# Gate o of an LSTM: its own PSUM bank and its own tanh, 1 + o on VectorE

## The chip, the cores and the metric

One core of a Trainium2 chip runs the whole program. The metric is the device time of one execution in microseconds (us), lower is better.

## The reference

The input x is (4, 64, 56, 56). Four stages follow, each with a residual: a layer norm over channels and an involution (7x7, 4 groups, kernels made from the pixel by two 1x1 convolutions); a top-2 mixture of 16 experts (SwiGLU, hidden 128); a 3x3 convolution; and an LSTM-like recurrence over the 3136 tokens of each of the 4 images, of which only this matters here:

```python
    def step(carry, xs):
        h, c = carry
        i_t = jax.nn.sigmoid(xi_t + h @ V_i)
        g_t = jnp.tanh(xg_t + h @ V_c)
        o_t = jax.nn.sigmoid(xo_t + h @ V_o)
        c_new = h * c + i_t * g_t
        h_new = o_t * jnp.tanh(c_new)
        return ((h_new, c_new), h_new)
    (_, _), hs = lax.scan(step, (h0, c0), (xi, xf, xg, xo))
```

(f_t is computed and not used.) Each token needs the h of the token before, so the 3136 steps can't overlap.

## The kernel before, in words

The image is worked off row by row, 56 rows of 56 pixels, 4 images side by side. All engines run the same schedule: a loop over rows whose body is unrolled over the 56 pixels t. In each step t an engine first does its part of the recurrence for pixel t of row j - 6 (LAG), and then its "fill", a piece of another stage for row j (pe_fill, act_fill, dve_fill). Which piece stands in which step is written by hand in main_places. Six head rows without recurrence come first, and the last six rows have no involution. Queues are in order; waits are semaphores, whose values are computed into registers (act_registers, fill_registers, pe_registers) inside the loop.

One step of the recurrence goes so. sigmoid(z) is (1 + tanh(z/2)) / 2, the halves are folded into the weights, and h is carried in two f16 digits: HR, and H5, the rest.

- TensorE (pe_row): when HR is written (hd1_done), three products VW x HR, for the gates g, i and o; when H5 is written (hd2_done), three products VB x H5. The first of each three is L1330, whose weights are loaded ahead, the two others are L1400. All add to one PSUM bank, GATES[c] (c = 0 for the first 28 pixels, 1 for the others), which already holds bias and input parts. The last product counts gates_done.
- ScalarE: L732 takes tanh of all three gates into G6 (4 images x 3, 12 elements). L736 then computes 1 + o twice into O5 (o1_done), and when the cell is there (cell_done) L739 takes tanh of it into TC5 in PSUM.
- VectorE (dve_row): L968, a scan, computes the cell from G6 and ADD3; then fill_registers; L975 takes the reciprocal of 1 + o when o1_done is there (rec_done); L979 writes HR = (1 + o) tanh(c); L982, a scan that needs the reciprocal, writes H5; L985 writes h to HIST; L987 the next ADD3.

The bias and input parts of the gates come from "prefill", nine products for each half row: three biases (L1116) and six input parts (L1120). Half 0 is prefilled in steps 51 to 54 (PRE0), half 1 in steps 3 and 6 (PRE1_AT). In step 6 a convolution tap (CONV, L1301) stands behind the prefill in TensorE's queue, in step 54 the duplication of the experts' input (DUP, L1158).

The experts' first product goes to bank H1B (H1, steps 12, 17, ..., 47) and is read by SI one step later; their second to H2B; the routing weights, spread by four products (L1269) in steps 14, 19, ..., 49, to bank DB, from which ScalarE copies them to DBS (L692) two steps later (the last time one step later). DB also takes the spread of the norm's scales (spread_rs, L1131, steps 10 and 11), copied by ScalarE in step 12 (RSC). L814 (RED, step 7) and L861 (DPLO, step 11) are fills of VectorE that work on 32 partitions beginning at 64 and at 32.

## Time and profile before

| what | value |
|---|---|
| three runs | 4000.49, 4002.73, 4004.25 us (median 4002.73) |
| the profiled execution, its own time | 4000.67 us |
| its span, first to last instruction | 3998.9 us |
| granted TensorE clock, mean | 0.517 |
| PE / PEld / DVE / ACT / POOL busy | 90 / 66 / 85 / 63 / 54 % |
| chain that ended last | PE 66%, DVE 14%, ACT 13%, issue 5%, POOL 1% |
| idle of ScalarE before L732, until TensorE's L1400 | 1195.7 us in 3073 of 3136 steps |
| idle of VectorE before L968, until L732 | 243.2 us in 874 steps |
| from 1000 to 2000 us: PE, PEld, DVE, ACT, POOL busy | 914, 676, 861, 652, 566 us, clock 0.50 |

The span is about 196 us of head rows and 3800 us of the loop, which looks the same from row to row. TensorE's busy share is high because its fills run while the recurrence is at ScalarE and VectorE; a matmul's record includes its latency, so that 90% isn't full use.

### The profile page before, as it was taken

What the parts mean: (1) busy time and instruction counts of PE and PEld (TensorE: products, weight loads), DVE (VectorE), ACT (ScalarE), POOL (GpSimd) and SP (SyncE); (2) the same over time, 40 slices, a digit from 0 to 9 for tenths busy, and PEclk for the clock granted to TensorE, in tenths of its full rate; (3) what the DMA queues carried; (4) which work ended last, traced back from release to release, by engine and by line L of the source; (5) the groups of instructions that cost most, each with busy time, mean ns of one, the idle gap of its engine ahead of it and who ended that gap; (6) DMA issues with size and microseconds to landing.
All of it is one profiled execution on the core that took longest, in us unless ns stands there. A gap on an engine that the chain in (4) does not pass through costs nothing.

```text
span 3998.9 us, 130353 instructions
## 1 busy us (share of the span) xinstructions
PE 3586.2 (90%) x35548; PEld 2658.7 (66%) x35548; DVE 3382.6 (85%) x21828; ACT 2526.5 (63%) x11666; POOL 2159.1 (54%) x3173
## 2 busy tenths in 40 slices
PE   6799999999898999999999999999989899988887
PEld 5666666666666666666666666666666666666665
DVE  6788888888888888888888888888888888887787
ACT  3366666666666666666666666666666666666565
POOL 6655565656565656555555555565655565652222
PEclk7955555555555555555555555555555555555555
DMA  5000000000000000000000000000000000000000
GB/s 74 2 1 1 1 1 1 1 1 1 1 1 1 1 1 1 1 1 1 1 1 1 1 1 1 1 1 1 1 1 1 1 1 1 1 2 1 1 1 1
DMA packets 44537, 11.06 MB, mean 3 GB/s; under 512 B 39913, under 2 KB 44010, under 8 KB 44490
## 3 DMA queue, kind: packets, MB, share of 16 engines
q1 hardware_dynamic: 42378, 10.05, 1.6%
q10 hardware_dynamic: 2112, 0.46, 0.1%
q8 instruction: 20, 0.33, 0.0%
q14 instruction: 27, 0.22, 0.0%
HBM read 7.29 MB, written 3.21 MB: 3 GB/s over the span
## 4 chain that ended last, share of the span: by engine, by line
PE 66%; DVE 14%; ACT 13%; issue 5%; POOL 1%; DVEq 0%; DMA 0%; ACTq 0%; POOLq 0%
PE GATES L1330 14%; PE YB L1150 10%; PE GATES L1400 9%; ACT O L736 7%; PE H1B L1144 7%; ACT G L732 6%; DVE O L975 6%; PE YB L1301 6%; PE TAPB L1137 6%; PE DB L1269 5%; DVE HR L979 5%; PE DB L1131 3%; PE H2B L1177 1%; PE H1B L1177 1%; PE H2B L1125 1%
## 5 line engine op out<-in xcount | busy, mean ns | idle before, releaser
L732 ACT ACTIVATE G<-GATES 128x12 f32<-128x12 f32 x3136 | 572.3, 182 | 1207.0 <-PE GATES L1400 1195.7
L1400 PEld LDWEIGHTS GATES<-HR,VW 128*128 128x128 f16 x6272 | 419.9, 106 | 605.7 <-issue 560.0
L968 DVE TENSOR_TENSOR_SCAN CT<-G,CT 128x12 f32<-128x12 f32 x3136 | 587.1, 187 | 268.0 <-ACT G L732 243.2
L1330 PE MATMUL GATES<-HR,VW 128*128 128x4 f16 x3136 | 532.2, 170 | 307.2 <-DVE HR L979 213.9
L736 ACT ACTIVATE O<-G 128x8 f32<-128x8 f32 x3136 | 662.1, 211 | 98.9 <-ACT G L732 0.2
L975 DVE RECIPROCAL O<-O 128x4 f32<-128x4 f32 x3136 | 567.5, 181 | 177.2 <-ACT O L736 0.2
L1396 PEld LDWEIGHTS <-VW 128*128 128x128 f16 x3136 | 457.4, 146 | 353.8 <-issue 317.2
L1400 PE MATMUL GATES<-H,VB 128*128 128x4 f16 x6272 | 616.8, 169 | 0.0
L987 DVE SCALAR_TENSOR_TENSOR CT<-HIST,CT 128x4 f32<-128x4 f32 x3136 | 521.4, 166 | 108.8
L1400 PE MATMUL GATES<-HR,VW 128*128 128x4 f16 x6272 | 613.1, 168 | 0.0
L1150 PE MATMUL YB<-HD,W 128*64 128x112 f32 x3840 | 595.5, 412 | 2.1 <-DVE HD L856 2.1
L530 POOL TENSOR_TENSOR HD<-VV,DBS 128x448 f32<-128x448 f32 x392 | 444.0, 1133 | 277.8 <-ACT DBS L692 277.8
L982 DVE TENSOR_TENSOR_SCAN H<-O,CT 128x20 f16<-128x20 f32 x3136 | 590.1, 188 | 0.0
L523 POOL TENSOR_TENSOR PA<-PA,XN 128x336 f32<-128x336 f32 x350 | 294.2, 841 | 446.7 <-ACT PA L659 446.7
L739 ACT ACTIVATE CT<-CT 128x8 f32<-128x8 f32 x3136 | 508.0, 162 | 40.0
L1330 PE MATMUL GATES<-H,VB 128*128 128x4 f16 x3136 | 525.4, 168 | 0.0
L979 DVE SCALAR_TENSOR_TENSOR HR<-O,CT 128x4 f16<-128x4 f32 x3136 | 498.4, 159 | 1.1
L1137 PE MATMUL TAPB<-RED,WT 128*128 128x112 f16 x2636 | 434.0, 283 | 2.2 <-DVE PD L842 2.0
L1144 PE MATMUL H1B<-XS,WM 128*128 128x224 f16 x1920 | 425.0, 375 | 0.0
L1144 PE MATMUL H2B<-XS,WM 128*128 128x224 f16 x1920 | 424.7, 375 | 0.2
L985 DVE TENSOR_TENSOR HIST<-O,CT 128x4 f32<-128x4 f32 x3136 | 415.8, 133 | 0.0
L1400 PEld LDWEIGHTS GATES<-H,VB 128*128 128x128 f16 x6272 | 414.7, 105 | 0.1
(242 smaller groups left out, 6995.0 us busy)
## 6 DMA issues: line engine op xcount, KB each, us to landing
out_dram<-OUT SPq DMA_DIRECT2D x112, 28.0 KB, 1.9
X<-in_x_dram SPq DMA_DIRECT2D x4, 672.0 KB, 11.3
STG<-in_L_ffn_w_dram SPq DMA_DIRECT2D x4, 512.0 KB, 12.5
U<-in_L_conv_U2s_dram SPq DMA_DIRECT2D x1, 972.0 KB
W<-in_L_ffn_w_dram SPq DMA_DIRECT2D x1, 512.0 KB, 11.7
X<-in_x_dram ACTq DMA_DIRECT2D x4, 112.0 KB, 3.0
S<-in_L_conv_S1s_dram SPq DMA_DIRECT2D x1, 108.0 KB
S<-in_L_conv_S2s_dram SPq DMA_DIRECT2D x1, 108.0 KB
```

The costliest lines, as they stand in the source:

```text
L732: act.activation(G6[:, :, 2:5], gates[c][:, w, :, :], ACT.Tanh, scale=1 / GSCALE).then_inc(step_in, 1)
L736: act.activation(O5[:, :, 1:5:3], G6[:, :, 3:4].broadcast_to([128, B, 2]), ACT.Copy, scale=O_MAX, bias=1.0)\
L968: dve.tensor_tensor_scan(CELL.rearrange("z b k -> z (b k)"), G6[:, :, :].rearrange("z b k -> z (b k)")[:, 0::2], ADD3.rearrange("z b k -> ...
L975: dve.reciprocal(O5[:, :, 3], O5[:, :, 1]).then_inc(rec_done, 1)
L979: dve.scalar_tensor_tensor(out=HR[:, :], in0=O5[:, :, 1], scalar=HSCALE, in1=TC5[:, :, 0], op0=ALU.mult, op1=ALU.mult)\
L982: dve.tensor_tensor_scan(H5[:, :, :].rearrange("z b k -> z (b k)"), O5[:, :, :].rearrange("z b k -> z (b k)"), TC5.rearrange("z b k -> z ( ...
L987: dve.scalar_tensor_tensor(out=ADD3[:, :, 2], in0=HIST[:, t, :], scalar=0.5, in1=CELL[:, :, 2], op0=ALU.mult, op1=ALU.mult).then_inc(step_ ...
L1137: last = pe.matmul(bank[:, m * TOK:(m + 1) * TOK], WT[:, i * K7 + j0 + m].rearrange("z p g c -> z (p g c)"), RED[:, :], start=(m == 0), st ...
L1144: last = pe.matmul(bank[:, m * 2 * TOK:(m + 1) * 2 * TOK], WM[:, which, part, EG * k + m, :], XS[:, :], start=(m == 0 and part == 0), stop ...
L1150: last = pe.matmul(YE[64 * p:64 * p + 64, :], W3[:, EG * k + m, :], HD[:, k % 2, m, p, :], start=first, stop=(k == NG - 1 and m == EG - 1) ...
L1330: return pe.add_instruction(mybir.InstMatmult(name=nc.get_next_instruction_name(), engine=mybir.EngineType.PE, start_tensor_calc=False, st ...
L1400: last = pe.matmul(gates[c][:, w, :, SLOT[g]], wt[:, g].rearrange("z m c -> z (m c)"), digit, start=False, stop=True, skip_group_check=True)
```

## The change

Gate o leaves the banks GATES and gets columns in bank DB (GATE_O, 112 columns for each half row), and OT, 4 more columns there, holds its tanh. Per step: TensorE counts gates_done after i's product with H5, the second of three, and gate_o_done after o's; ScalarE takes tanh of g and i into G6 (8 elements), then tanh of o into OT (4 elements, PSUM to PSUM), and L736 is gone; VectorE, behind the cell's scan, waits for OT and computes 1 + o twice into O5 (8 elements), and only then does its registers and the reciprocal.

Around it: the spread scales of the norm go to H2B and the routing weights to H1B instead of DB, so that H1 waits for the copy DBS (dbs_done) instead of SI, and H2 for the copy of the scales (rsc_done). The nine prefill products come in another order, o's three last: in step 6 for half 1 and in step 54 for half 0, and the first of them waits for o1_done of the same step. Since bank DB can't be cleared while it is in use, ScalarE writes zeros to the other half's GATE_O behind L739 in steps 1 and 49, and o's product with HR in steps 2 and 50 waits for that (oz_done). In the head rows DB is used as before.

```diff
-        PRE0={51: (0, 1, 2), 52: (3, 4), 53: (5, 6), 54: (7, 8)}, COPY=None, RSE=None)
+        PRE0={51: (0, 1), 52: (2, 3), 53: (4, 5), 54: (6, 7, 8)}, COPY=None, RSE=None)
...
-PRODUCTS = 3 + 2 * 3
-PRE1_AT = {3: (0, 1, 2, 3, 4), 6: (5, 6, 7, 8)}
-SLOT = (2, 0, 1)
+
+INPUTS = (("b", 0), ("b", 1), (0, 0), (0, 1), (1, 0), (1, 1), ("b", 2), (0, 2), (1, 2))
+PRODUCTS = len(INPUTS)
+FIRST_O = INPUTS.index(("b", 2))
+PRE1_AT = {3: (0, 1, 2, 3, 4, 5), 6: (6, 7, 8)}
+ZERO_AT = (1, 49)
+SLOT = (1, 0)
 MAIN, HEAD = main_places(), head_places()
...
-        gates = [g[:, 0:HALF * B * 3].rearrange("z (k b t) -> z t b k", b=B, k=3) for g in GATES]
+        gates = [g[:, 0:HALF * B * 2].rearrange("z (k b t) -> z t b k", b=B, k=2) for g in GATES]
+        GATE_O = [DB[:, c * TOK:(c + 1) * TOK] for c in range(2)]
+        gate_o = [g.rearrange("z (b t) -> z t b", b=B) for g in GATE_O]
+        OT = DB[:, 448:448 + B]
...
         def spread(lstm):
-            return DB if lstm else GATES[1]
+            return H2B if lstm else GATES[1]
+
+        def weights_bank(lstm):
+
+            return H1B if lstm else DB
 
...
-                act.activation(DBS[:, :], DB[:, 0:EG * 2 * TOK], ACT.Copy).then_inc(dbs_done, 1)
+                act.activation(DBS[:, :], weights_bank(lstm)[:, 0:EG * 2 * TOK], ACT.Copy).then_inc(dbs_done, 1)
...
                     act.wait_ge(gates_done, 1 + n + 1)
-                    act.activation(G6[:, :, 2:5], gates[c][:, w, :, :], ACT.Tanh, scale=1 / GSCALE).then_inc(step_in, 1)
+                    act.activation(G6[:, :, 2:5:2], gates[c][:, w, :, :], ACT.Tanh, scale=1 / GSCALE).then_inc(step_in, 1)
+                    act.wait_ge(gate_o_done, 1 + n + 1)
+                    act.activation(OT[:, :], gate_o[c][:, w, :], ACT.Tanh, scale=1 / GSCALE).then_inc(ot_done, 1)
                     act_registers(act, j, t, involution)
-
-                    act.wait_ge(step_in, 1 + 2 * n + 2)
-                    act.activation(O5[:, :, 1:5:3], G6[:, :, 3:4].broadcast_to([128, B, 2]), ACT.Copy, scale=O_MAX, bias=1.0)\
-                        .then_inc(o1_done, 1)
                     act.wait_ge(cell_done, 1 + n + 1)
                     act.activation(TC5[:, :, 0:4:3], CELL[:, :, 2:3].broadcast_to([128, B, 2]), ACT.Tanh, scale=0.5)\
                         .then_inc(t_done, 1)
+                    for k in range(2):
+                        if t == ZERO_AT[k]:
+
+                            act.wait_ge(o1_done, 1 + n + 1)
+                            act.activation(GATE_O[1 - k], CST[:, CZERO:CZERO + 1].broadcast_to([128, TOK]), ACT.Copy).then_inc(oz_done, 1)
                 act_fill(act, j, t, involution, lstm, experts, pre)
 
         def act_head_row(act, j):
...
+                    dve.wait_ge(ot_done, 1 + n + 1)
+                    dve.scalar_tensor_tensor(out=O5[:, :, 1:5:3], in0=OT[:, :].unsqueeze(2).broadcast_to([128, B, 2]), scalar=O_MAX,
+                                             in1=O5[:, :, 2:3].broadcast_to([128, B, 2]), op0=ALU.mult, op1=ALU.subtract)\
+                        .then_inc(o1_done, 1)
                     fill_registers(dve, j, t, involution, lstm, experts)
...
-        def prefill(pe, c, k):
-
-            if k < 3:
-                return pe.matmul(GATES[c][:, SLOT[k] * TOK:(SLOT[k] + 1) * TOK], BX[:, k].rearrange("z m c -> z (m c)"),
-                                 ONEH[:, :], start=(k == 0), stop=False, skip_group_check=True)
-            d, g = divmod(k - 3, 3)
+        def prefill(pe, c, k, lstm):
+
+
+            d, g = INPUTS[k]
+            bank = GATE_O[c] if g == 2 else GATES[c][:, SLOT[g] * TOK:(SLOT[g] + 1) * TOK]
+            if d == "b":
+                return pe.matmul(bank, BX[:, g].rearrange("z m c -> z (m c)"), ONEH[:, :],
+                                 start=(k == 0 or (k == FIRST_O and not lstm)), stop=False, skip_group_check=True)
             xs = X4S[:, :].rearrange("z (p q w) -> z p q w", p=2, q=Q)[:, :, :, c * HALF:(c + 1) * HALF]
-            return pe.matmul(GATES[c][:, SLOT[g] * TOK:(SLOT[g] + 1) * TOK].rearrange("z (q p t) -> z p q t", q=Q, p=2),
+            return pe.matmul(bank.rearrange("z (q p t) -> z p q t", q=Q, p=2),
...
                         if lstm:
-                            pe.wait_ge(dbs_done, 1 + NG * j)
+
+                            pe.wait_ge(ve_done, 1 + 2 * j + 2)
...
-                    last = prefill(pe, 1, k)
+                    if k == FIRST_O:
+                        pe.wait_ge(o1_done, 1 + (j - LAG) * W + t + 1)
+                    last = prefill(pe, 1, k, lstm)
                     if k == PRODUCTS - 1:
                         last.then_inc(pre1_done, 1)
             if experts and t in P.H1:
                 k = P.H1.index(t)
-                pe.wait_ge(si_done, 1 + NG * j + k)
+                if lstm:
+                    pe.wait_ge(dbs_done, 1 + NG * j + k)
+                else:
+                    pe.wait_ge(si_done, 1 + NG * j + k)
...
-                    pe.wait_ge(ve_done, 1 + 2 * j + 2)
+                    pe.wait_ge(rsc_done, 1 + j + 1)
...
-                    if lstm:
-                        pe.wait_ge(rsc_done, 1 + j + 1)
                     pe.wait_ge(dp_step, 1 + 3 * j + 3)
                 for m in range(EG):
                     for p in range(2):
-                        last = pe.matmul(DB[:, (2 * m + p) * TOK:(2 * m + p + 1) * TOK], SEL[:, p, EG * k + m, :], DP[:, :],
+                        last = pe.matmul(weights_bank(lstm)[:, (2 * m + p) * TOK:(2 * m + p + 1) * TOK], SEL[:, p, EG * k + m, :], DP[:, :],
...
-                    last = prefill(pe, 0, k)
+                    if k == FIRST_O and lstm:
+                        pe.wait_ge(o1_done, 1 + (j - LAG) * W + t + 1)
...
-                if experts:
+                if experts and lstm:
+                    pe.wait_ge(dbs_done, 1 + NG * (j + 1))
+                elif experts:
...
+            if t - 1 in ZERO_AT:
+                pe.to_reg(1 + 2 * (j - LAG) + ZERO_AT.index(t - 1) + 1)
...
-                pe.to_reg(1 + NG * j)
+                pe.to_reg(1 + 2 * j + 2)
...
+            if FIRST_O in PRE1_AT.get(t, ()) or FIRST_O in P.PRE0.get(t, ()):
+                pe.to_reg(1 + (j - LAG) * W + t + 1)
...
                         multiply_loaded(pe, gates[c][:, w, :, SLOT[0]], first, digit)
-                        for g in range(1, 3):
-                            last = pe.matmul(gates[c][:, w, :, SLOT[g]], wt[:, g].rearrange("z m c -> z (m c)"), digit,
-                                             start=False, stop=True, skip_group_check=True)
-                    last.then_inc(gates_done, 1)
+                        last = pe.matmul(gates[c][:, w, :, SLOT[1]], wt[:, 1].rearrange("z m c -> z (m c)"), digit,
+                                         start=False, stop=True, skip_group_check=True)
+                        if wt is VB:
+                            last.then_inc(gates_done, 1)
+                        if wt is VW and t - 1 in ZERO_AT:
+                            pe.wait_ge(oz_done, 1 + 2 * (j - LAG) + ZERO_AT.index(t - 1) + 1)
+                        last = pe.matmul(gate_o[c][:, w, :], wt[:, 2].rearrange("z m c -> z (m c)"), digit,
+                                         start=False, stop=True, skip_group_check=True)
+                    last.then_inc(gate_o_done, 1)
```

## Rows read from the trace of the kernel before

**Rows 1.** The page, the chain that ended last, shares of the span by engine

```profile
PE 66%; DVE 14%; ACT 13%; issue 5%; POOL 1%; DVEq 0%; DMA 0%; ACTq 0%; POOLq 0%
```

**Rows 2.** One line of the kernel, L732: duration ns min/median/max, first and last start

```profile
L732 ACT ACTIVATE G<-GATES x3136: 182/182/185, 196.2 to 3993.6; 128x12 f32<-128x12 f32 x196
```

**Rows 3.** Timeline of a quiet step (step 18 of a row): start us, duration us, instruction

```profile
2251.44 0.18 ACT L732 ACTIVATE G<-GATES 128x12 f32<-128x12 f32 x1 [0.61 <-PE GATES L1400]
2251.65 0.19 DVE L968 TENSOR_TENSOR_SCAN CT<-G,CT 128x12 f32<-128x12 f32 x1
...
2251.87 0.16 ACT L739 ACTIVATE CT<-CT 128x8 f32<-128x8 f32 x1
2251.89 0.18 DVE L975 RECIPROCAL O<-O 128x4 f32<-128x4 f32 x1
2251.95 0.54 ACT L687 ACTIVATE SI<-H1B 128x448 f32<-128x448 f32 x1
2252.07 0.16 DVE L979 SCALAR_TENSOR_TENSOR HR<-O,CT 128x4 f16<-128x4 f32 x1
...
2252.14 0.19 DVE L982 TENSOR_TENSOR_SCAN H<-O,CT 128x20 f16<-128x20 f32 x1
2252.25 0.13 DVE L985 TENSOR_TENSOR HIST<-O,CT 128x4 f32<-128x4 f32 x1
...
2252.38 0.17 PE L1330 MATMUL GATES<-H,VB 128*128 128x4 f16 x1
...
2252.41 0.20 PE L1400 MATMUL GATES<-H,VB 128*128 128x4 f16 x2
2252.41 0.17 DVE L987 SCALAR_TENSOR_TENSOR CT<-HIST,CT 128x4 f32<-128x4 f32 x1
...
2252.64 0.18 ACT L732 ACTIVATE G<-GATES 128x12 f32<-128x12 f32 x1 [0.16 <-PE GATES L1400]
```

**Rows 4.** The page, costliest groups: busy us, mean ns of one | idle before

```profile
L975 DVE RECIPROCAL O<-O 128x4 f32<-128x4 f32 x3136 | 567.5, 181 | 177.2 <-ACT O L736 0.2
```

**Rows 5.** Timeline of TensorE's products in step 6, the tap behind the prefill

```profile
2237.03 0.73 PE L1301 MATMUL YB<-N,WC 128*128 x2
```

**Rows 6.** Timeline of step 19, first weight load, four products, H's first product

```profile
2252.60 0.32 PEld L1269 LDWEIGHTS DB<-DP,SEL 128*128 128x128 f16 x4
2252.63 0.53 PE L1269 MATMUL DB<-DP,SEL 128*128 128x112 f16 x4
...
2253.60 0.17 PE L1330 MATMUL GATES<-H,VB 128*128 128x4 f16 x1
```

**Rows 7.** Timeline of TensorE's products in step 54, two prefills and the four duplications

```profile
2294.73 0.35 PE L1120 MATMUL GATES<-X4S,UX 128*128 128x112 f16 x2
2294.87 0.58 PE L1158 MATMUL H1B<-XD,IDUP 128*128 128x112 f16 x4
```

**Rows 8.** Timeline of VectorE between step 7 and step 8

```profile
2239.08 0.17 DVE L987 SCALAR_TENSOR_TENSOR CT<-HIST,CT 128x4 f32<-128x4 f32 x1
2239.28 0.27 DVE L814 TENSOR_TENSOR RED<-TAPB,RED 32x112 f16<-32x112 f32 x1
2239.58 0.19 DVE L968 TENSOR_TENSOR_SCAN CT<-G,CT 128x12 f32<-128x12 f32 x1
```

**Rows 9.** Timeline of VectorE between step 11 and step 12

```profile
2243.97 0.17 DVE L987 SCALAR_TENSOR_TENSOR CT<-HIST,CT 128x4 f32<-128x4 f32 x1
2244.16 0.26 DVE L861 TENSOR_TENSOR DP<-TAPB,DH 32x112 f16<-32x112 f32 x1
```

**Rows 10.** Timeline of VectorE in the first step of a row

```profile
2230.13 0.18 DVE L975 RECIPROCAL O<-O 128x4 f32<-128x4 f32 x1
...
2230.34 0.20 DVE L982 TENSOR_TENSOR_SCAN H<-O,CT 128x20 f16<-128x20 f32 x1
```

**Rows 11.** Timeline of step 17, a step with address work: scan and reciprocal

```profile
2250.45 0.19 DVE L968 TENSOR_TENSOR_SCAN CT<-G,CT 128x12 f32<-128x12 f32 x1
...
2250.69 0.18 DVE L975 RECIPROCAL O<-O 128x4 f32<-128x4 f32 x1
```

More of the change, by code:

```diff
@@ L278, in build_program @@
             "conv_done slot3_done slot2_done res4a_done res4_done")
-        (dupx_done, x4_done, pre0_done, pre1_done, gates_done, step_in, o1_done, cell_done,
+        (dupx_done, x4_done, pre0_done, pre1_done, gates_done, gate_o_done, oz_done, step_in, ot_done, o1_done, cell_done,
          t_done, rec_done, hd1_done, hd2_done, h_done, ocopy_done, oadd_done, ostored) = lstm_sems = sems(
-            "dupx_done x4_done pre0_done pre1_done gates_done step_in o1_done cell_done "
+            "dupx_done x4_done pre0_done pre1_done gates_done gate_o_done oz_done step_in ot_done o1_done cell_done "
             "t_done rec_done hd1_done hd2_done h_done ocopy_done oadd_done ostored")
@@ L1275, in pe_fill @@
                         pe.wait_ge(x4_done, 1 + j + 1)
-                    last = prefill(pe, 0, k)
+                    if k == FIRST_O and lstm:
+                        pe.wait_ge(o1_done, 1 + (j - LAG) * W + t + 1)
+                    last = prefill(pe, 0, k, lstm)
                     if k == PRODUCTS - 1:
@@ L1451, in _ @@
             pe.wait_ge(lead_rs, RSN)
-            spread_rs(pe, spread(True), 0, LEAD).then_inc(lead_rsb, 1)
+            spread_rs(pe, DB, 0, LEAD).then_inc(lead_rsb, 1)
             pe.wait_ge(bns_set, 1)
```

## The prediction

> **What bounds the kernel now.** First the chain that ended last: TensorE, VectorE and ScalarE take turns and nothing else counts [rows 1]. Then the line of the gate activation, L732: it ran 3136 times, first at 196.2 and last at 3993.6 us, one in (3993.6 - 196.2) / 3135 = 1.211 us [rows 2]. So 3136 steps of a recurrence fill 3798 of 3998.9 us, and the question is what one step costs. Then one quiet step in the timeline [rows 3], counted from the start of L732 (call it 0): scan L968 at 0.21, cell tanh L739 at 0.43, HR (first digit of h) at 0.63, H (second digit, L982) at 0.70, its first product L1330 at 0.94, the other two within 0.06 more, next L732 at 1.20. Two bystanders matter: L736 (1 + o) ends when the scan does, and the reciprocal starts at 0.45 and ends at 0.63, landing near 0.67, 0.03 before H. The rows are rounded to 0.01; I carry a third digit from groups of them and take 1.207 for a step without a disturbance; the rest of the 1.211 is the row starts and a few steps named below. TensorE was granted 0.50, that is 1.2 GHz, in every stretch of the loop, and I keep that.
>
> **What the step gains.** (a) L732 no longer waits for o's last product. Three products start within 0.06 us (the pair's record is 0.20 long, one is 0.17), so one is worth 0.028. (b) L732 reads 8 instead of 12 elements: 0.003. (c) L736 goes, but L739 waits for the scan anyway (L968 ends at 0.40, L739 starts 0.03 later): 0. (d) The new tanh of o: ScalarE starts SI (L687) 0.08 after a tanh of 0.16 began [rows 3], so it starts at about 0.09, ends at about 0.25, lands at 0.28. It hides beside the scan.
>
> **What it loses: 1 + o and the reciprocal.** VectorE now computes 1 + o behind the scan. When may it start? After the H scan the next instruction starts 0.11 later, after HR 0.07 [rows 3]; bounds 0.07 and 0.11, I take 0.10 since it follows a scan of 12 elements where the H scan has 20. It lasts like L987, 0.17, or like HR, 0.16, both of 4 elements [rows 3]; I take 0.163. From end to a waiting VectorE instruction 0.034 (L985 ends at 2252.38, L987 starts at 2252.41). So: 0.211 + 0.097 + 0.163 + 0.034 = 0.505 for the reciprocal, + 0.181 [rows 4] + 0.034 = **0.720 for H, against 0.706 now**: it becomes the bound of H, 0.014 late. HR stays at 0.63. The step: 0.720 + 0.241 to its first product + 0.026 to the second + 0.205 to L732 = **1.192, 0.015 less**. 3136 x 0.015 = **-47 us**. With the bounds for start and length the step gives back between 0.033 (then the cell tanh sets H) and 0: -104 to 0.
>
> **What it loses once a row** (56 rows). TensorE's queue is in order, and two of its fills get a wait for 1 + o of the same step. o1 lands at 0.505, but a fill starts right behind the last product, at -0.18.
> - Step 6: three prefill products of o wait from -0.18 to 0.51. Behind them stands a convolution tap [rows 5], and behind that the next step's six products. In step 19 the weight load of four such products starts at 2252.60, the four end at 2253.16, a tap follows, and the H product comes at 2253.60 [rows 6]: 1.00 from first load to H product; with three products 0.91. So the H product comes at 0.51 + 0.91 = 1.42 instead of 0.96: +0.46, less what makes today's step 6 0.01 long already, which the delay covers: +0.455, 56 x 0.455 = **+25.5**.
> - Step 54: the same wait, three products, then four duplications. A product of 112 columns adds 0.09 (four last 0.53, two 0.35) [rows 6, 7]. 0.51 + 0.03 + 7 x 0.093 = 1.19, and 0.08 to the H product (in step 19 it starts 0.08 before the tap's record ends): 1.27, +0.31, x 56 = **+17.4**.
> - Steps 19, 24, 29, 34, 39 hold four products and a tap and are bound by TensorE already, by 0.007. There the earlier L732 buys nothing: 280 x 0.0165 = **+4.6**.
> - Step 8 and step 12 follow VectorE instructions on 32 partitions, L814 (50 rows) and L861 (56). L814 starts 0.20 behind the start of L987 where others start 0.08 behind, and the scan waits for its end, 0.30 behind its start [rows 8]; L861 starts 0.19 behind L987 [rows 9]. A change of partitions waits for the end of what went before. The first instruction that writes SBUF from partition 0 again is now 1 + o. If it waits for the scan's end it starts 0.12 later and all of that counts. Bounds 0 and 0.12; I take 0.12, as three of the four changes in the rows wait: 106 x 0.12 = **+12.7**. L814 also pushes the scan 0.033 further past a step that is shorter: +1.7.
> - Row start: the reciprocal is late today and H follows its end by 0.03 [rows 10]. Its registers must now be read before 1 + o too: +0.047 x 56 = +2.6.
>
> The Trainium skill (VectorE: DVE Perf Modes, Two Vector instructions with no wait between them) says that an instruction is held until all before it are done if it writes a memory from another quadrant than the last writer of that memory did. By it the 12.7 is certain, and without it the sum is 12.7 less; no row of this kernel shows the case of two instructions back.
>
> **Registers.** The register work of VectorE moves behind 1 + o. It isn't in the rows. In a step with address work (14 a row, 50 rows) the reciprocal starts 0.24 behind the scan, as elsewhere [rows 11], so the work fits into 0.24. It now starts when o's tanh has landed (0.28) and may end at 0.49 to 0.52, the reciprocal being due at 0.505. Bounds 0 and 0.08 (the row start's lateness) in 700 steps; I take 0.005: +3.5.
>
> **Costed at nothing.** PRE0 and PRE1 only move products. Expert input H1 now waits for the copy DBS, which ends about 1.05 in the step before and lands at 1.08, while H1 would start at 1.02. Four products of 224 columns and a tap are 9 x 0.093 = 0.84 from 1.08: 0.71 of the next step, and HR ends at 0.79 there; covered, in all 7 steps a row. RSB's spread uses H2B, and H2 waits for its copy in the same way. Both zeroings of the o bank (ScalarE, steps 1 and 49) start at 0.51, last some 0.3 and end before o's product at 0.89. If ScalarE were late there, 0.1 x 112 = 11 us.
>
> **Sum.** -47.0 + 25.5 + 17.4 + 4.6 + 12.7 + 1.7 + 2.6 + 3.5 = **+21 us**. The profiled execution took 4000.67 (span 3998.9); the median of the runs is 4002.7, 2 more. So 4024.
>
> **Rivals.**
> 1. *Faster: the reciprocal isn't what H waits for.* The point is whether 1 + o starts and lasts no more than 0.24 together (mine: 0.26). If VectorE may start it 0.07 behind the scan, as behind HR, H falls back to the cell tanh and the step is 1.174: -104; the row's losses are then bigger, +88 (each of them counts from an H 0.018 earlier, and the registers up to 13). 4003 - 16 = 3987. For: 0.07 is seen many times. Against: never behind a scan. 0.15.
> 2. *Faster: the two waits cost little*, because o1 comes earlier or the fills are short. Without the 25.5 and 17.4 the sum is -22: 3981. Against: the queue is in order and the rows' lengths stand. 0.04.
> 3. *Slower: the registers start only when 1 + o starts*, at 0.31 not 0.28, and delay the reciprocal by 0.04 in 700 steps: +27, 4051. 0.12. Or the step gains nothing (both bounds high): +62, 4065. 0.06.
> 4. *VectorE does not overlap at all here*: 1 + o would start at the scan's end, 0.09 later, 3136 times: +282, 4306. Against: HR and H overlap by half in every step [rows 3]. 0.02. The Trainium skill (same page, The DRAIN you can't avoid) first has it that the next instruction does not start until the pipe is empty, and then that one which isn't held starts earlier; by the first this rival, by the second my 0.10. The trace agrees with the second: 0.07 behind the start of an instruction of 0.16.
> 5. *The change doesn't bite*: o's bank keeps L732 waiting and the step stays 1.207 with the losses of the row: 4065, counted above.
>
> **How the numbers follow.** Forecast 0.61, its own range 4008 to 4042. The range 3984 to 4055 reaches to rival 1 and to rival 3's first case, and leaves the others out. Within 0.2% means within 8 us, about what a measurement of this kernel can tell from none: 0.13, from the forecast's low end (if steps 8 and 12 aren't held) and from between it and rival 1. Faster 0.19 (rivals 1, 2), slower 0.68.
>
> **What would show it.** Right: L732 to L732 in a quiet step 1.19; the reciprocal at 0.50, H at 0.72, 0.03 behind the reciprocal's end; TensorE idle for some 0.6 in steps 6 and 54 and these steps 0.45 and 0.31 long; 1 + o 0.22 instead of 0.10 behind the scan in steps 8 and 12. Wrong: H at 0.70 (rival 1); no idle stretch in step 6; a quiet step of 1.21.

## The result, and the profile after

| | before | after |
|---|---|---|
| median, us | 4002.98 | 4101.86 |
| the profiled execution, its time and span | 4000.67, 3998.9 | 4100.99, 4099.2 |
| first L732 / L744 to the last | 3797.4 | 3896.1 |
| chain that ended last | PE 66%, DVE 14%, ACT 13% | DVE 69%, PE 16%, ACT 5% |

The ratio is 1.025 (1.023 to 1.026): 2.5% slower. One of the four executions after was a slow one, 5576.7 us at a granted clock of 1.0, and the median and the ratio are of the other three. The sign was forecast, the size was not: 4102 is 78 above the forecast of 4024 and outside its range. Nearly all of the difference lies in the 3136 steps of the recurrence (3896.1 - 3797.4 = 98.7 us of the 100.3 between the spans). Lines have moved: L732 is now L744, L968 is L983, L975 is L995, L979 is L999, L982 is L1002, L985 is L1005, L987 is L1007, L739 is L749; new are L746 (tanh of o) and L988 (1 + o).

The page of the kernel after: the span, VectorE's share among the busy times, part 3 (DMA queue: packets, MB, share of 16 engines), the chain by engine and by line, and four groups (busy us, mean ns of one | idle before).

```profile
span 4099.2 us, 133498 instructions
...
q14 instruction: 274, 2.24, 0.2%
...
DVE 69%; PE 16%; issue 8%; ACT 5%; POOL 1%; DVEq 0%; DMA 0%; ACTq 0%; POOLq 0%
DVE O L995 12%; DVE CT L983 9%; DVE O L988 8%; DVE CT L1007 8%; DVE HR L999 7%; DVE H L1002 7%; DVE VV L846 6%; PE GATES L1360 6%; DVE PD L857 4%; ACT G L744 4%; DVE HIST L1005 3%; PE GATES L1433 2%; PE H2B L1153 1%; PE H2B L1147 1%; PE H1B L1166 1%
...
L744 ACT ACTIVATE G<-GATES 128x8 f32<-128x8 f32 x3136 | 566.8, 181 | 1249.0 <-PE GATES L1433 1200.4
...
L995 DVE RECIPROCAL O<-O 128x4 f32<-128x4 f32 x3136 | 567.9, 181 | 139.4 <-DVE O L988 20.6
...
L1002 DVE TENSOR_TENSOR_SCAN H<-O,CT 128x20 f16<-128x20 f32 x3136 | 613.9, 196 | 0.0
...
L988 DVE SCALAR_TENSOR_TENSOR O<-DB,O 128x8 f32<-128x8 f32 x3136 | 495.4, 158 | 3.3
```

The chain [rows 1] went to VectorE, which fits the forecast that the reciprocal behind 1 + o sets H. The line to stop at is the queue of code, which the page calls "instruction" (q14); its row in the page of before is this:

```profile
q14 instruction: 27, 0.22, 0.0%
```

Ten times as many packets of code are fetched after the change. Between 1000 and 2000 us, which is 14 to 15 rows of the loop, the queue has no row at all before and this one after:

```profile
q14 instruction: 72, 0.59, 0.2%
```

So before, none falls into the loop between its first row and its last; after, five of 8192 bytes fall into each row.

A quiet step (step 18, as in [rows 3]) in the kernel after; ScalarE and VectorE, and H's products:

```profile
2312.34 0.18 ACT L744 ACTIVATE G<-GATES 128x8 f32<-128x8 f32 x1 [0.61 <-PE GATES L1433]
2312.42 0.17 ACT L746 ACTIVATE DB<-DB 128x4 f32<-128x4 f32 x1
2312.56 0.19 DVE L983 TENSOR_TENSOR_SCAN CT<-G,CT 128x12 f32<-128x12 f32 x1
2312.66 0.16 DVE L988 SCALAR_TENSOR_TENSOR O<-DB,O 128x8 f32<-128x8 f32 x1
...
2312.85 0.18 DVE L995 RECIPROCAL O<-O 128x4 f32<-128x4 f32 x1
...
2312.98 0.16 DVE L999 SCALAR_TENSOR_TENSOR HR<-O,CT 128x4 f16<-128x4 f32 x1
2313.07 0.20 DVE L1002 TENSOR_TENSOR_SCAN H<-O,CT 128x20 f16<-128x20 f32 x1
...
2313.31 0.17 PE L1360 MATMUL GATES<-H,VB 128*128 128x4 f16 x1
...
2313.55 0.18 ACT L744 ACTIVATE G<-GATES 128x8 f32<-128x8 f32 x1 [0.15 <-PE GATES L1433]
```

The step is as forecast: 1 + o 0.10 behind the scan, reciprocal 0.50 and H 0.72 behind L744, next L744 at 1.20 (means of many rows; single rows are rounded to 0.01). So the loss is in single steps. Their lengths (us from the start of L744, or L732, to the next one; medians over rows 2 to 49; in brackets the last six rows, which are a loop of their own with less work):

| step | before | after | forecast of after |
|---|---|---|---|
| quiet | 1.207 | 1.197 | 1.192 |
| 0 | 1.307 (1.33) | **1.988** (1.40) | 1.34 |
| 6 | 1.220 (1.21) | 1.754 (1.65) | 1.66 |
| 8 | 1.260 (1.21) | 1.416 (1.20) | 1.40 |
| 12 | 1.207 (1.21) | 1.332 (1.33) | 1.31 |
| 14 | 1.207 (1.21) | **1.285** (1.20) | 1.19 |
| 27 | 1.207 (1.21) | **1.576** (1.20) | 1.20 |
| 54 | 1.207 (1.21) | 1.508 (1.51) | 1.50 |

Steps 0, 14 and 27 lose 1.1 us a row that no step of the prediction holds, and only in the rows of the 50-row loop. VectorE's timeline there, at the row's start (L1007 of the last step, scan and 1 + o of the first) and in step 27:

```profile
2288.68 0.17 DVE L1007 SCALAR_TENSOR_TENSOR CT<-HIST,CT 128x4 f32<-128x4 f32 x1
2289.85 0.19 DVE L983 TENSOR_TENSOR_SCAN CT<-G,CT 128x12 f32<-128x12 f32 x1 [1.00 <-ACT G L744]
2289.98 0.17 DVE L988 SCALAR_TENSOR_TENSOR O<-DB,O 128x8 f32<-128x8 f32 x1
...
2323.45 0.16 DVE L988 SCALAR_TENSOR_TENSOR O<-DB,O 128x8 f32<-128x8 f32 x1
2324.03 0.18 DVE L995 RECIPROCAL O<-O 128x4 f32<-128x4 f32 x1 [0.41 <-DVE O L988]
```

The scan of step 0 begins 1.17 behind L1007 (0.50 in the kernel before, where L987 starts at 2229.31 and L968 at 2229.81). The profile names L744 as what ended the wait, but L744 had begun at 2288.88 and lasts 0.18; VectorE's own queue was late. The row of the loop's branch shows it, L1126 after (between 2287.5 and 2291 us) and L1106 before (between 2228.5 and 2231 us), each with the instruction that comes next in VectorE's queue:

```profile
L1126 DVEq COMPARE_BRANCH  x1: 68/68/68, 2288.8 to 2288.8; - x1
L1126 DVEq BRANCH_PREFETCH_HINT  x1: 45/45/45, 2289.7 to 2289.7; - x1
```

```profile
L1106 DVEq COMPARE_BRANCH  x1: 61/61/61, 2229.4 to 2229.4; - x1
L1106 DVEq BRANCH_PREFETCH_HINT  x1: 39/39/39, 2229.7 to 2229.7; - x1
```

From the start of the branch to the start of the next instruction it is 0.26 before and 0.92 in this row after (0.85 in the median of the rows), with no wait in between. In step 27 the reciprocal starts 0.42 after 1 + o has ended, and the profile puts that down to 1 + o itself, which was done.

**Theory A**: the change adds one VectorE instruction to each of the 56 unrolled steps; the loop's body grows from 463 to 520 instructions of the compiled program, too many to be kept from one row to the next, so it is fetched again in every row. **Theory B**: these steps are late by the new wait and by the registers behind it.

### The profile page after: what moved, and what is told of

Its sections match the earlier page's. It is cut to its first block, busy times and chain, and to the rows that moved or that the text cites. A ratio compares the mean times of both kernels' runs of the same rounds, so it can differ in the third digit from the quotient of the medians.

```text
span 4099.2 us, 133498 instructions
## 1 busy us (share of the span) xinstructions
PE 3651.4 (89%) x35548; PEld 2753.2 (67%) x35548; DVE 3471.5 (85%) x24964; ACT 2094.2 (51%) x11778; POOL 2154.1 (53%) x3173
## 4 chain that ended last, share of the span: by engine, by line
DVE 69%; PE 16%; issue 8%; ACT 5%; POOL 1%; DVEq 0%; DMA 0%; ACTq 0%; POOLq 0%
DVE O L995 12%; DVE CT L983 9%; DVE O L988 8%; DVE CT L1007 8%; DVE HR L999 7%; DVE H L1002 7%; DVE VV L846 6%; PE GATES L1360 6%; DVE PD L857 4%; ACT G L744 4%; DVE HIST L1005 3%; PE GATES L1433 2%; PE H2B L1153 1%; PE H2B L1147 1%; PE H1B L1166 1%
## 5 line engine op out<-in xcount | busy, mean ns | idle before, releaser
L744 ACT ACTIVATE G<-GATES 128x8 f32<-128x8 f32 x3136 | 566.8, 181 | 1249.0 <-PE GATES L1433 1200.4
L983 DVE TENSOR_TENSOR_SCAN CT<-G,CT 128x12 f32<-128x12 f32 x3136 | 586.3, 187 | 313.4 <-ACT G L744 299.1
L749 ACT ACTIVATE CT<-CT 128x8 f32<-128x8 f32 x3136 | 508.0, 162 | 625.7 <-DVE CT L983 622.1
L1360 PE MATMUL GATES<-HR,VW 128*128 128x4 f16 x3136 | 543.9, 173 | 293.5 <-DVE HR L999 223.4
L1433 PEld LDWEIGHTS GATES<-HR,VW 128*128 128x128 f16 x3136 | 348.0, 111 | 564.8 <-issue 497.1
L995 DVE RECIPROCAL O<-O 128x4 f32<-128x4 f32 x3136 | 567.9, 181 | 139.4 <-DVE O L988 20.6
L1007 DVE SCALAR_TENSOR_TENSOR CT<-HIST,CT 128x4 f32<-128x4 f32 x3136 | 522.2, 167 | 108.8
L1002 DVE TENSOR_TENSOR_SCAN H<-O,CT 128x20 f16<-128x20 f32 x3136 | 613.9, 196 | 0.0
L746 ACT ACTIVATE DB<-DB 128x4 f32<-128x4 f32 x3136 | 542.0, 173 | 1.2
L1433 PE MATMUL GATES<-H,VB 128*128 128x4 f16 x3136 | 532.1, 170 | 0.0
L1433 PE MATMUL GATES<-HR,VW 128*128 128x4 f16 x3136 | 530.8, 169 | 0.0
L1439 PE MATMUL DB<-H,VB 128*128 128x4 f16 x3136 | 529.1, 169 | 0.0
L1439 PE MATMUL DB<-HR,VW 128*128 128x4 f16 x3136 | 526.9, 168 | 0.0
L1360 PE MATMUL GATES<-H,VB 128*128 128x4 f16 x3136 | 525.6, 168 | 0.0
L988 DVE SCALAR_TENSOR_TENSOR O<-DB,O 128x8 f32<-128x8 f32 x3136 | 495.4, 158 | 3.3
L999 DVE SCALAR_TENSOR_TENSOR HR<-O,CT 128x4 f16<-128x4 f32 x3136 | 491.5, 157 | 0.0
L1166 PE MATMUL H1B<-XS,WM 128*128 128x224 f16 x1920 | 433.6, 379 | 0.0
## 6 DMA issues: line engine op xcount, KB each, us to landing
STG<-in_L_ffn_w_dram SPq DMA_DIRECT2D x4, 512.0 KB, 12.7
```

The source lines that it names most:

```text
L744: act.activation(G6[:, :, 2:5:2], gates[c][:, w, :, :], ACT.Tanh, scale=1 / GSCALE).then_inc(step_in, 1)
L746: act.activation(OT[:, :], gate_o[c][:, w, :], ACT.Tanh, scale=1 / GSCALE).then_inc(ot_done, 1)
L983: dve.tensor_tensor_scan(CELL.rearrange("z b k -> z (b k)"), G6[:, :, :].rearrange("z b k -> z (b k)")[:, 0::2], ADD3.rearrange("z b k -> ...
L988: dve.scalar_tensor_tensor(out=O5[:, :, 1:5:3], in0=OT[:, :].unsqueeze(2).broadcast_to([128, B, 2]), scalar=O_MAX, in1=O5[:, :, 2:3].broad ...
L995: dve.reciprocal(O5[:, :, 3], O5[:, :, 1]).then_inc(rec_done, 1)
L999: dve.scalar_tensor_tensor(out=HR[:, :], in0=O5[:, :, 1], scalar=HSCALE, in1=TC5[:, :, 0], op0=ALU.mult, op1=ALU.mult)\
```

## The experiments

All runs, medians in us, beside the kernel before on the same chip (4001.6 to 4003.6). "Body" is VectorE's instructions in the 50-row loop, "packets" those of queue 14.

| run | body | packets | median | ratio to before |
|---|---|---|---|---|
| before | 463 | 27 | 4003.0 | |
| e2, before + 40 waits | 503 | 27 | 4008.9 | 1.002 (1.001 to 1.003) |
| e8, before + 49 waits | 512 | 274 | 4122.2, one run | |
| e9, before + 50 waits | 513 | 274 | 4119.9, one run | |
| e1, before + 56 waits | 519 | 274 | 4097.3 | 1.024 (1.022 to 1.025) |
| after | 520 | 274 | 4101.9 | 1.025 (1.023 to 1.026) |
| e6, after, short body | 508 | 27 | 4051.2 | 1.012 (1.011 to 1.014) |
| e12, after, registers packed | 510 | 29 | 4049.5 | 1.012 (1.010 to 1.013) |
| e3, after, o last | 520 | 274 | 4077.4 | 1.019 (1.017 to 1.021) |
| e10, e6 with o last | 508 | 27 | 4005.4 | 1.001 (1.000 to 1.002) |
| e11, e12, o last, DP swapped | 510 | 29 | 3998.2 | 0.999 (0.998 to 1.000) |
| e7, after, DPLO from partition 0 | 520 | 275 | 4095.2, one run | |
| e4, after, 1 + o on ScalarE | 463 | 30 | 4181.4 | 1.045 (1.043 to 1.047) |
| e5, e4 with o last | 463 | 29 | 4139.1 | 1.034 (1.032 to 1.036) |

### Code that is longer and does nothing more (e1, e2, e8, e9)

```diff
                     dve.tensor_tensor(HIST[:, t, :], ...).then_inc(h_done, 1)
+                    if involution and t < 56:
+                        dve.wait_ge(set_dve, 1)
                     dve.wait_ge(h_done, 1 + n + 1)
```

The wait is on a semaphore that was counted long ago. e2 has 40, e8 49, e9 50 in place of 56.

> The kernel before, with one satisfied wait more ahead of ADD3 in each of the 56 steps of the 50-row loop: no work is added, VectorE's loop body grows from 463 to 519 instructions (the kernel after has 520). Theory A (a loop body of VectorE over some limit between 491 and 519 instructions is fetched again in every row, and steps 0, 14 and 27 wait for it): some 1.06 us in each of 49 rows, about +50 us, 4045 to 4065 us; queue 14 'instruction' of the page some 270 packets instead of 27; step 0 of a row about 0.6 us longer. Theory B (those steps of the kernel after are late because of 1 + o's wait and of the registers behind it, not by the size of the code): within 8 us of the kernel before (the waits lie beside HIST), 27 packets.

> The same waits in the first 40 steps only, 503 instructions in VectorE's loop body. Theory A with a limit near 512 instructions: within 6 us of the kernel before, 27 packets of instructions. Theory A with a limit below 503: like the run with 519, +50 us. Theory B: within 6 us. A third reading, C (each satisfied wait itself costs time in its step): 40/56 of what the run with 519 loses, some +36 us.

> The kernel before with 49 satisfied waits a row, 512 instructions in VectorE's loop body. 503 and 508 were fetched once, 519 and 520 in every row. If the limit is 512: 27 packets in queue 14 and some 4009 us; if it is lower, some 270 packets and over 4080 us.

> The same with 50 waits a row, 513 instructions. If the limit is 512: some 270 packets and over 4080 us; if the limit lies higher (513 to 518): 27 packets and some 4009 us.

In e1, part 3 of the page, and VectorE around the start of a row:

```profile
q14 instruction: 274, 2.24, 0.2%
```

```profile
2288.45 0.17 DVE L989 SCALAR_TENSOR_TENSOR CT<-HIST,CT 128x4 f32<-128x4 f32 x1
2290.36 0.19 DVE L968 TENSOR_TENSOR_SCAN CT<-G,CT 128x12 f32<-128x12 f32 x1 [1.75 <-issue]
```

Here the profile says "issue": nothing that it shows was waited for. Step 0 is 2.793 long (+1.49), step 27 +0.19, steps 14 and 41 +0.04 and +0.06; with 0.13 below that is 1.9 us a row, 50 x 1.9 = 95 of the 96 us. Theory A had step 0 longer by 0.6 and 4045 to 4065 us: the packets came as expected, the price was nearly twice that. Of e2:

```profile
q14 instruction: 27, 0.22, 0.0%
```

e2 costs 7 us: step 8 is 0.073 and step 29 0.053 longer, so the satisfied waits cost something only there; step 0 is 1.307 as before, and reading C (36 us) falls. Sixteen waits more cost 88, and between e2 and e8 nine waits more cost 113. Theory B can't explain a kernel with no 1 + o on VectorE. The limit, expected at 512, is lower: a body of 512 is fetched again (e8) and one of 510 is not (e12). These two are different kernels, and 511 was not tried.

### The kernel after with a shorter body (e6, e12)

e6 leaves out 8 instructions VV, two DM, one maximum and one index a row, and with them a part of the output (e10, further down, does too). e12 leaves nothing out:

```diff
+                if involution and k < NT and t == P.PROD[k][0] - 1:
+                    dve.to_reg(1 + 2 * NT * j + 2 * k + 1)
+                    dve.to_reg(1 + 2 * NT * j + 2 * k + 2)
                 if involution and k < NT and t in P.PROD[k]:
                     h = P.PROD[k].index(t)
-                    dve.to_reg(1 + 2 * NT * j + 2 * k + h + 1)
                     dve.lower_ap(window(j, k, 2 * h, 2))
```

The compiled program puts several register operations into one instruction; most steps need one such instruction, the 14 steps of PROD and step 0 needed a second.

> The kernel after, with VectorE's loop body cut from 520 to 508 instructions: the first half of the product VV (8 instructions a row) and the gating's maximum, index and two DM of the first position are left out, so those parts of the output are not computed; all else stands, 1 + o and its wait too. Theory A with a limit near 512: steps 0, 14 and 27 of a row go back to about 1.40, 1.20 and 1.20 us, 27 packets of instructions, and the time falls by 50 to 65 us, to 4040 to 4055 us. Theory B: steps 0 and 27 stay at 2.0 and 1.58 us, and the time falls by under 10 us, to 4093 to 4104 us. If the limit is below 508, it stays too, with some 270 packets.

> The kernel after with nothing left out: the register values of the 14 products PROD are computed one or two steps earlier, in steps whose register instruction has room, so that ten register instructions fewer are needed and VectorE's loop body has 510 instructions instead of 520. Theory A (re-fetched code, 53 us by the run with 508): 27 packets in queue 14, steps 0, 14 and 27 at 1.38, 1.20 and 1.21 us, 4043 to 4055 us. Theory B (these steps are late by 1 + o's wait and by the register work as such): the amount of register work is the same, so within 10 us of the kernel after.

e12: part 3 of the page, then VectorE in step 0 (scan, 1 + o) and step 27 (1 + o, reciprocal), where L985, L990 and L997 are L983, L988 and L995:

```profile
q14 instruction: 29, 0.24, 0.0%
```

```profile
2256.85 0.19 DVE L985 TENSOR_TENSOR_SCAN CT<-G,CT 128x12 f32<-128x12 f32 x1 [0.31 <-ACT G L744]
2256.98 0.17 DVE L990 SCALAR_TENSOR_TENSOR O<-DB,O 128x8 f32<-128x8 f32 x1
...
2290.34 0.16 DVE L990 SCALAR_TENSOR_TENSOR O<-DB,O 128x8 f32<-128x8 f32 x1
2290.53 0.18 DVE L997 RECIPROCAL O<-O 128x4 f32<-128x4 f32 x1
```

Steps 0, 14 and 27 are 1.372, 1.200 and 1.201. With the same arithmetic the recurrence (first L744 to last) takes 52 us less, and 49 in e6, where these three steps give back 53 (1.06 a row) and a quiet step is 1.200 instead of 1.197. Packing the registers also takes some 0.02 from steps such as 16, 36 and 41, some 6 us in all. Theory A stands, theory B falls.

The trace also has the start of each packet, and with it the price at the row's start can be read. All times are us, medians over the rows of the loop; the branch is L1126 or its like, and times of a packet are from the branch's start:

| run | body | first packet of the turn | next instruction of VectorE | from packet to instruction | step 0 |
|---|---|---|---|---|---|
| before | 463 | none | 0.26 | | 1.307 |
| e12 | 510 | none | 0.23 | | 1.372 |
| after | 520 | -0.94 | 0.85 | 1.77 | 1.988 |
| e3 | 520 | -0.63 | 1.15 | 1.77 | 2.286 |
| e1 | 519 | -0.15 | 1.66 | 1.78 | 2.793 |
| e9 | 513 | 0.43 | 2.21 | 1.77 | 3.266 |
| e8 | 512 | 0.47 | 2.23 | 1.77 | 3.280 |

In all five kernels with packets, VectorE goes on 1.77 to 1.78 us after the first packet of the turn has begun, though the branch lies anywhere from 0.94 behind that packet's start to 0.47 ahead of it. The kernel after pays only 0.6 a row of it, since its packet begins 0.94 ahead of the branch; e1 and e8 pay 1.4 and 2.0 for the same 1.77. So the kernels with satisfied waits cost more than theory A had expected. What decides when the first packet begins is open, and so is which packet the stalls of steps 14 and 27 belong to.

### The two waits of the prefill (e3, e10)

```diff
                 pe_fill(pe, j, t, involution, lstm, experts, pre)
+                if lstm:
+                    prefill_o(pe, j, t, pre)
```

prefill_o issues what pe_fill now skips: o's three products of the half, the first with its wait for 1 + o.

> The kernel after, with o's three products of the prefill moved to the end of TensorE's other work in steps 6 and 54, so that what TensorE does in those steps does not wait behind 1 + o. The prediction's price of the two waits (0.455 and 0.31 us a row, 56 rows, 43 us): step 54 falls from 1.508 to about 1.20 us and step 6 from 1.754 to about 1.20 to 1.30 us, in all some 0.8 us a row, 4055 to 4065 us. Rival (the two steps are long by the load of the prefill itself and the wait only shows it): within 10 us of the kernel after, 4090 to 4104 us. Steps 0, 14 and 27 stay as in the kernel after by theory A and by theory B.

> The run with 508 instructions in VectorE's loop (4051 us) and o's prefill products last in steps 6 and 54. If the 0.30 us a row that step 0 took back in the run with 520 instructions is the fetch of code becoming the limit, it isn't there now: 4051 - 43 = 4008 us (4003 to 4013). If step 0 is longer for another reason (a prefill that ends later), 26 us less: 4025 us.

Step 54 fell to 1.200 and step 6 to 1.295, 0.77 us a row, or 43 us; yet e3 gained 24 (4101.9 to 4077.4), between the forecast and its rival. Step 0 had grown from 1.988 to 2.286: the branch comes 0.30 earlier against the first packet (0.63 behind its start instead of 0.94), and VectorE still goes on 1.77 behind the packet, so that the 0.30 which step 54 no longer loses is lost there. That is 15 us. Another 6 or so are a quiet step of 1.200 instead of 1.197, for which nothing was tried. In e10, with no code to fetch, the gain is 4051.2 - 4005.4 = 46 us. The costs of the wait and of the code overlap, so parts taken from one kernel don't add up in another.

### Steps 8 and 12, and all three at once (e7, e11)

```diff
+        DL = sb("DL", [2 * E, TOK], F16)
...
-                dve.tensor_tensor(DP[32:64, :], dispatch(lstm), DH[:, :], ALU.subtract).then_inc(dp_step, 1)
+                dve.tensor_tensor(DL[0:32, :] if lstm else DP[32:64, :], dispatch(lstm), DH[:, :], ALU.subtract).then_inc(dp_step, 1)
```

> The kernel after, with step 11's DPLO of VectorE writing its 32 partitions to another SBUF tile from partition 0 instead of DP from partition 32 (the low digit of the dispatch is left out of the experts' weights that way); its length and place in the queue stay. The prediction's reading (1 + o is held until all before it are done, as VectorE's last write to SBUF began at another partition): step 12 falls from 1.331 to 1.20 us, 7.5 us in all, 4090 to 4096 us. Rival (step 12 is long as DPLO itself stands in VectorE's queue, or its input is late): step 12 stays at 1.33 us, 4101 us. Step 8, where RED is not changed, stays at 1.415 us in both.

VectorE from step 11's DPLO to step 12's 1 + o, in the kernel after (L876 writes from partition 32) and in e7 (L877, from partition 0):

```profile
2304.69 0.17 DVE L1007 SCALAR_TENSOR_TENSOR CT<-HIST,CT 128x4 f32<-128x4 f32 x1
2304.89 0.26 DVE L876 TENSOR_TENSOR DP<-TAPB,DH 32x112 f16<-32x112 f32 x1
2305.11 0.19 DVE L983 TENSOR_TENSOR_SCAN CT<-G,CT 128x12 f32<-128x12 f32 x1
2305.32 0.17 DVE L988 SCALAR_TENSOR_TENSOR O<-DB,O 128x8 f32<-128x8 f32 x1
```

```profile
2300.46 0.17 DVE L1008 SCALAR_TENSOR_TENSOR CT<-HIST,CT 128x4 f32<-128x4 f32 x1
2300.53 0.25 DVE L877 TENSOR_TENSOR DL<-TAPB,DH 32x112 f16<-32x112 f32 x1
2300.87 0.19 DVE L984 TENSOR_TENSOR_SCAN CT<-G,CT 128x12 f32<-128x12 f32 x1
2300.97 0.16 DVE L989 SCALAR_TENSOR_TENSOR O<-DB,O 128x8 f32<-128x8 f32 x1
```

1 + o starts 0.21 behind the scan's start (0.02 behind its end) in the first and 0.10 in the second, DPLO itself starts 0.07 instead of 0.20 behind L1007 (L1008 in e7), and step 12 is 1.200. Step 8 stayed at 1.415. What holds 1 + o in step 12 is the partition from which DPLO writes, not its length. Step 8 has the same form (RED, from partition 64) and was not tried.

e11 is e12 with o last and with the digits of DP exchanged:

```diff
-                for dst in (DP, DH):
-                    act.activation(dst[0:2 * E, :], dispatch(lstm), ACT.Copy).then_inc(dp_step, 1)
+                for dst in (DP[32:64, :] if lstm else DP[0:32, :], DH[:, :]):
+                    act.activation(dst, dispatch(lstm), ACT.Copy).then_inc(dp_step, 1)
...
-                dve.tensor_tensor(DP[32:64, :], dispatch(lstm), DH[:, :], ALU.subtract).then_inc(dp_step, 1)
+                dve.tensor_tensor(DP[0:32, :] if lstm else DP[32:64, :], dispatch(lstm), DH[:, :], ALU.subtract).then_inc(dp_step, 1)
```

> The run before this one, with o's prefill products last in steps 6 and 54 (46 us where the code isn't re-fetched: 4051 to 4005) and with the two digits of DP changing places, so that VectorE writes step 11's digit from partition 0 (step 12 at 1.20 instead of 1.33 us, 7.5 us; ScalarE then writes 32 partitions from 32 in step 10, where nothing of its own is due). All three costs named so far are out: 4101 - 53 - 46 - 7.5 = 3994 us (3988 to 4002), level with or just under the kernel before (4003). Rival (ScalarE's own hold in step 10 or 11 costs what VectorE's saved): 4002 us.

3998.2, ratio 0.999 (0.998 to 1.000): the step of 1.20 at last shows, and pays for what remains (steps 0, 6 and 8 are 1.369, 1.295 and 1.419). Computing everything, it is level with the kernel before, at best two tenths of a per cent faster.

### 1 + o back on ScalarE (e4, e5)

```diff
+                    act.wait_ge(step_in, 1 + 2 * n + 2)
+                    act.wait_ge(ot_done, 1 + n + 1)
+                    act.activation(O5[:, :, 1:5:3], OT[:, :].unsqueeze(2).broadcast_to([128, B, 2]), ACT.Copy, scale=O_MAX, bias=1.0)\
+                        .then_inc(o1_done, 1)
                     act.wait_ge(cell_done, 1 + n + 1)
...
-                    dve.wait_ge(ot_done, 1 + n + 1)
-                    dve.scalar_tensor_tensor(out=O5[:, :, 1:5:3], in0=OT[:, :].unsqueeze(2).broadcast_to([128, B, 2]), scalar=O_MAX,
-                                             in1=O5[:, :, 2:3].broadcast_to([128, B, 2]), op0=ALU.mult, op1=ALU.subtract)\
-                        .then_inc(o1_done, 1)
```

> The kernel after with 1 + o back on ScalarE (behind the tanh of o, ahead of the cell tanh), VectorE's loop body at 463 instructions again, its registers behind the scan. Measured so far: the re-fetching of VectorE's code costs 53 us (520 against 508 instructions), steps 8 and 12 some 0.155 and 0.134 us a row (16 us), the registers behind 1 + o some 7 us. If each of these goes, 4101 - 76 = 4025 with the step left at 1.197 us. As 1 + o then lands at about 0.46 to 0.48 instead of 0.50, the reciprocal sets H 0.02 to 0.03 earlier and a quiet step is 1.17 to 1.18: 3950 to 3975 us. Rival: 1 + o on ScalarE pushes the cell tanh behind it, a quiet step stays at 1.20 or more: 4015 to 4040 us. Steps 6 and 54 keep their wait in both. Queue 14: 27 packets.

> The run before this one with o's prefill products last in TensorE's work of steps 6 and 54. With VectorE's code not re-fetched, the whole gain of that move should show, 0.454 + 0.308 us a row as steps 6 and 54 showed it (the run with 520 instructions gave 0.30 of it back in step 0): 40 to 45 us below the run before this one, 3905 to 3935 us by the first reading, 3970 to 4000 by the rival. Alternative: the 0.30 in step 0 is given back here too, whatever the code's size: only 25 us below.

ScalarE and the reciprocal in a quiet step of e4:

```profile
2349.08 0.18 ACT L744 ACTIVATE G<-GATES 128x8 f32<-128x8 f32 x1 [0.66 <-PE GATES L1432]
2349.15 0.17 ACT L746 ACTIVATE DB<-DB 128x4 f32<-128x4 f32 x1
2349.42 0.18 ACT L750 ACTIVATE O<-DB 128x8 f32<-128x8 f32 x1
2349.51 0.16 ACT L753 ACTIVATE CT<-CT 128x8 f32<-128x8 f32 x1
```

```profile
2349.63 0.18 DVE L994 RECIPROCAL O<-O 128x4 f32<-128x4 f32 x1 [0.15 <-ACT O L750]
```

Both readings missed. The cell tanh was not pushed (0.43 behind L744 as before), but 1 + o starts only 0.10 after o's tanh has ended (0.34 behind L744; on VectorE 0.31) and lasts 0.18 (0.16 there). It waits for two semaphores here; whether that is what delays it was not tried. The reciprocal starts 0.55 behind L744, so the step is 1.246 and 3136 x 0.049 = 154 us are lost. Steps 17 and 34, where 1 + o starts another 0.09 to 0.10 later, lose 9 more, and against that stand some 84 saved (code, steps 8 and 12, registers): 79 net, 79.5 measured. The packets fell to 30, as A says. e5 is 42 us below e4, as expected, and its step 0 is 1.310 as e4's: the alternative (0.30 given back whatever the code's size) falls.

## Why the prediction was wrong in size

| term, us | predicted | measured |
|---|---|---|
| quiet step | -47.0 | -30 (0.0095 x 3136) |
| step 6, the wait | +25.5 | +30 |
| step 54, the wait | +17.4 | +17.4 |
| steps 19 to 39 bound by TensorE | +4.6 | -1.4 |
| steps 8 and 12 held | +12.7 + 1.7 | +15.7 |
| row start | +2.6 | +4.6 (e6) |
| registers behind 1 + o | +3.5 | +8 |
| **code fetched again in every row** | not considered | **+53** |
| sum | +21 | +97 (loop: +98.7) |

The measured terms are a step's length minus before's, plus the 0.0095 already counted for every step, times its rows (step 54: (0.302 + 0.0095) x 56). The +53 is what steps 0, 14 and 27 are longer than in e6.

- **The missing step.** The sum said +21; its own terms, as measured, give +44. The other 53 are the code of VectorE. The prediction counted each added instruction's time and never their number, though the change adds one to each of 56 unrolled steps: the fetch of VectorE's code is missing from its sum and from "Costed at nothing", and no rival named it either. With the body at 510 the same kernel takes 4049, inside the range. The Trainium skill (Runtime: NRT & Kernel Launch, Instruction fetch mechanics) has it that most engines keep 512 instructions (TensorE 2048) and that a taken branch to code no longer there stalls until it is fetched. By it a body of 520 is fetched again and one of 463 is not, and the runs agree; a body of 512 would just fit, and here the measurement differs (e8, 274 packets). The price (53 us and more) is known from the runs alone.
- **Quiet step: right mechanism, too large a gain.** The reciprocal is the bound (chain 69% VectorE), 1 + o starts and lasts as taken (0.10, 0.16), and H starts 0.716 behind L744 (0.720 forecast). But H's scan is 0.196 long, as it was when the reciprocal held it up at the row's start [rows 10], and not the 0.19 of [rows 3], and its product follows 0.249 instead of 0.241 behind. 1.197, not 1.192: 17 us, the largest mis-sized term. The 0.003 for 8 elements instead of 12 was 0.001 (182 to 181 ns).
- **The two waits: right, step 6 a little too small.** TensorE is idle in step 6 until 1 + o and the step is 0.53 longer instead of 0.455. The rest is on ScalarE:

```profile
2296.35 0.40 ACT L665 ACTIVATE TAPB<-TAPB,BN 32x112 f32<-32x112 f32 x1
...
2296.93 0.18 ACT L744 ACTIVATE G<-GATES 128x8 f32<-128x8 f32 x1 [0.18 <-PE GATES L1433]
2297.14 0.16 ACT L746 ACTIVATE DB<-DB 128x4 f32<-128x4 f32 x1
2297.14 0.19 DVE L983 TENSOR_TENSOR_SCAN CT<-G,CT 128x12 f32<-128x12 f32 x1
2297.33 0.17 DVE L988 SCALAR_TENSOR_TENSOR O<-DB,O 128x8 f32<-128x8 f32 x1
...
2297.55 0.28 PE L1139 MATMUL DB<-ONEH,BX 128*128 128x112 f16 x1 [0.63 <-DVE O L988]
```

  Two instructions earlier L665 wrote PSUM from partition 64, and o's tanh, the first to write PSUM from partition 0 again, starts 0.21 behind L744 (0.08 in the quiet step), when L744 has ended. In the last six rows, without L665, step 6 is 0.10 shorter. That it is the partition is argued from VectorE's case and was not tried alone.
- **Steps 8 and 12: right**, 0.16 and 0.135, and e7 shows the reason for step 12. The Trainium skill (VectorE: DVE Perf Modes, Two Vector instructions with no wait between them) states this hold, and goes by the last output into that memory, however many instructions back; in e7, where it lies two back, the trace agrees.
- **Steps 19 to 39: wrong.** They are 1.199, no longer than others; the 1.213 of before is gone. What had bound them before stays open.
- **Registers: too small.** The heavy steps are 0.00 to 0.03 longer than quiet ones (steps 16, 31, 36 and 41: 1.226, 1.219, 1.220, 1.219), some 0.165 a row.
- **Costed at nothing: held.** Steps 1, 49, 2, 50 and the steps of H1 and H2 show no stall.

Of the signs named, those for "right" came true but for two sizes: step 6 is 0.53 longer instead of 0.45, and the quiet step is 1.197 instead of 1.19. None of them looks at the row's start or at the instruction queue, where the miss lay.

## What to carry to other kernels

Before adding an instruction to an unrolled loop, count the body: on this engine 510 instructions ran without being fetched again and 512 did not, and going over cost 1.3 to 2.8%, more than the added instructions' own time. The two were different kernels, so leave a few instructions of room. The count of packets in the queue of instructions shows it at once, as does a stall that returns once per iteration and is missing in a shorter loop of the same code; register work packed into fewer instructions is a way back under. A gain of 0.01 us a step is easily outweighed by a few longer steps a row, so list these before the average.

## What the runs showed of the hardware that was not expected

- The profile names no cause for code being fetched: in the kernel after it put the wait down to L744, in e1 to "issue".
- The same re-fetch (274 packets) cost 53 us in the kernel after, but 88 to 113 in those made longer by waits (step 0: 1.99, 2.79 in e1, 3.28 in e8). In each, VectorE went on 1.77 us after the first packet of a row's turn had begun; the price at the row's start is what of that lies behind the branch.
- Five packets a row for 520 instructions: they came in steps 55, 0, 14, 28 and 41 (the first at the row's turn, the others some 13.5 steps of 9.3 instructions apart, so about 126 instructions). Within the row the stalls and the packets don't coincide: in step 27 the reciprocal starts 0.88 behind L744, the packet 1.78. So for steps 14 and 27 the runs show that the fetch costs the time (both stalls are gone in e6 and e12), not which packet ends which stall.
